# An audio tower on one core: the first normalisation is formed by ACT from PSUM, and DVE applies gamma and beta over pairs of blocks

## The chip, the cores and the metric

The kernel runs on one core of a Trainium2 chip. The metric is the device time of one execution in microseconds (us). TensorE (PE in the profile, PEld for its weight loads) does the matmuls, VectorE (DVE) and ScalarE (ACT) the elementwise work, GpSimd (POOL) a few small operations and the indirect DMAs, SyncE (SP) issues the other DMAs. Each engine works through its own program in order and waits on semaphores.

## What is computed

```python
# tokenizer: patches of 16 time steps, projected, then normalised with gamma and beta
y = einsum('bpi,di->bpd', patches, W) + b
mu, var = mean(y), mean((y - mu)**2)
h = (y - mu) * rsqrt(var + 1e-5) * gamma + beta
# layer 0
h = h + attention(layernorm(h))      # one head, 124 tokens for each batch entry
h = h + ffn(layernorm(h))            # router, top 2 of 6 experts, each of three 256x256 layers
```

There are 128 batch entries of 124 tokens, with 256 features, all in float32. The change concerns the normalisation of the tokenizer only, the line that forms `h`.

## The kernel before

The program has two parts. Part A runs `pipeline(step)`: 36 iterations, `it` = 0 to 35, over 32 groups of four batch entries (a block is one entry: 124 tokens on the partitions, 256 features along them). It is a software pipeline of depth 5. In iteration `it` the stage x0 works on group `it` (tokenizer, its normalisation, the second normalisation), x1 on group `it`-1 (transposed activations, q and v), x2 on `it`-2 (scores, softmax, attention output), x3 on `it`-3 (third normalisation, router), x4 on `it`-4 (top two, places of the tokens in the experts' tables), x5 on `it`-5 (the rest of its scatters). Part B runs `tiles`: 67 tiles of 512 rows through the experts' three layers. It begins when all rows have been scattered, and the change doesn't touch it.

What order the engines follow is written out by hand, in one `step` function per engine; nothing else sets it. The piece around the change, on each engine:

- PE writes the projection of a group into banks 6 and 7, two blocks of 256 columns in each (L550 to L555), and counts `tok_ps`. Later in the same iteration it writes v of the group before into the same banks (L637 to L648), when DVE has read them.
- DVE takes the statistics of the four blocks from PSUM (`statistics(0, ...)`, L889 and L892), which gives mean and variance in `mv`. It goes on with `gates` and `place` (L967) of stage x4. `place` waits for PE's position counts, and PE's transposes of the probabilities (L605) wait for `place`, since both use bank 4.
- POOL forms `rstd1`, the inverse standard deviation, with two small operations (L413, L416), then issues three scatters (L424), and later the same two operations for `rstd2`.
- DVE then forms `y = (x - mean) * gamma` from PSUM (L975, four instructions) and `h = y * rstd + beta` (L981, four), takes the statistics of `h`, and goes on to `nmr` of the second normalisation (L1010) and the attention residual of x2 (L1018).
- ACT copies the transposed probabilities (`pT`, L792), forms `rhT` of the router (L796) and the high half of a weight chunk (L801), and then waits for `nmr` to form the second normalisation `xn1` (L808), which PE transposes (L527) ahead of the scores (L536).

`ln1` counts DVE's steps on a group in stage x0: 25 per group before.

Of the kernel before, what the change touches and what calls it, by code (L numbers as in the profile page):

```python
# [24 lines left out]
ALU = mybir.AluOpType  # L25
# [3 lines left out]
P = 128  # L29
# [29 lines left out]
LN1_N, AV_N, TOPK_N, POS_N = 25, 14, 25, 4  # L59
# [17 lines left out]
def audio_tower(nc, x, tok_w, tok_b, tok_gamma, tok_beta, wq, bq, wk, bk, wv, bv, scale,  # L77
                rw1, rb1, rw2, rb2, eweights, esmall, out):
    with ExitStack() as ctx:
# [39 lines left out]
        nmr = sb("nmr", [P, 2, GB])  # L119
# [37 lines left out]
        with ExitStack() as part_a:  # L157
# [33 lines left out]
            "w_high", "w_low", "dummy_cleared", "xT_high", "xT_low", "xn1T_low", "tok_ps", "ln1", "rstd1", "rstd2", "rstd3", "xn1_ready", "xn1T_ps", "xn1T_sb",  # L191
# [187 lines left out]
        def _(pool):  # L379
# [48 lines left out]
            def step(it, group_of):  # L428
                x0, x2, x4, x5 = (group_of(s) for s in (0, 2, 4, 5))
                if x0:  # L430
                    g, slot, rnd = x0
                    wait_apart(pool, S["ln1"], g * LN1_N + 2 * GB, S["pool_passed"])
                    inverse_std(0, S["rstd1"], g)
                if x5:
                    scatter(x5[0], range(3, 6))
                if x0:
                    g, slot, rnd = x0
                    wait(pool, S["xn1_ready"], g * GB)
                    wait_apart(pool, S["ln1"], g * LN1_N + 6 * GB, S["pool_passed"])
                    inverse_std(1, S["rstd2"], g)  # L440
                if x5:
                    scatter(x5[0], range(6, 8))
                if x2:
                    g, slot, rnd = x2
                    wait(pool, S["xn2_ready"], g * GB)
                    wait_apart(pool, S["av"], g * AV_N + 1 + 3 * GB, S["pool_passed"])
                    inverse_std(2, S["rstd3"], g)
                if x4:
                    g, slot, rnd = x4
                    pool.wait_ge(S["pos"], (g + 1) * POS_N)  # L450
                    pool.wait_ge(S["topk"], (g + 1) * TOPK_N)
                    wait_apart(pool, S["xn2_ready"], (g + 1) * GB, S["pool_passed"])
                    scatter(g, range(3 if g < G - 1 else GB * TOPK))
# [27 lines left out]
        def _(pe):  # L481
# [37 lines left out]
            def step(it, group_of):  # L519
# [19 lines left out]
                if x0:  # L539
# [5 lines left out]
                    for pair in range(2):  # L545
                        bank_read(pe, (S["v_ready"], it - 2, (it - 2) * 2 + pair + 1),
                                  (S["ln1"], it - 1, (it - 1) * LN1_N + 2 * GB + 2 + 2 * pair))
# [89 lines left out]
                if x1:  # L637
                    g, slot, rnd = x1
                    for pair in range(2):
                        bank_read(pe, (S["ln1"], it, it * LN1_N + 2 * GB + 2 + 2 * pair),  # L640
# [61 lines left out]
        def _(act):  # L702
# [26 lines left out]
            def step(it, group_of):  # L729
# [59 lines left out]
                if x2:  # L789
                    g, slot, rnd = x2  # L790
                    act.wait_ge(S["pT_ps"], g + 1)
                    act.activation(pT[0:TOK + 1, :], banks[4][0:TOK + 1, 0:GT], ACT.Identity).then_inc(S["pT_sb"], 1)  # L792
                if x3:
# [66 lines left out]
        def _(v):  # L860
# [21 lines left out]
            def statistics(which, src, s, at, g):  # L882

                for j in range(GB):
                    if which == 0:
                        v.wait_ge(S["tok_ps"], g * 2 + j // 2 + 1)
                    else:
# [35 lines left out]
            def step(it, group_of):  # L923
# [35 lines left out]
                if x4:  # L959
                    gates(*x4)  # L960
                if x4:
# [8 lines left out]
                if x0:  # L970
                    g, slot, rnd = x0
                    at = g * LN1_N
                    v.wait_ge(S["rstd1"], g * 2 + 2)
                    for j in range(GB):
                        v.scalar_tensor_tensor(out=y[R, j, :], in0=embedded(j), scalar=mv[R, 0, j, 0:1],  # L975
                                               in1=gamma_bc[R, :], op0=ALU.subtract, op1=ALU.mult).then_inc(S["ln1"], 1)
                    wait(v, h2_stored[slot], rnd * 16)
                    wait(v, S["xn2_ready"], (g - RING + 1) * GB)
                    for j in range(GB):
                        v.wait_ge(S["ln1"], at + 2 * GB + 1 + j)  # L980
                        v.scalar_tensor_tensor(out=h[R, slot, j, :], in0=y[R, j, :], scalar=rstd[R, 0, j:j + 1],  # L981
                                               in1=beta_bc[R, :], op0=ALU.mult, op1=ALU.add).then_inc(S["ln1"], 1)
                if x0:
                    g, slot, rnd = x0
                    statistics(1, lambda j: h[R, slot, j, :], S["ln1"], g * LN1_N + 4 * GB, g)
# [238 lines left out]
```

## Time and profile before

| | us |
|---|---|
| median of 3 runs | 1405.89 (1405.25 to 1407.78) |
| the profiled execution | 1404.13 |
| its span, first to last instruction | 1402.3 |
| outside the span | 1.8 |

| engine | busy us | share of the span |
|---|---|---|
| PE | 1250.8 | 89% |
| PEld | 1088.5 | 78% |
| DVE | 1057.7 | 75% |
| POOL | 925.9 | 66% |
| ACT | 841.6 | 60% |

Part A fills the span up to about 700 us, part B the rest. A share of busy time is a mean over both, so the rows are best read part by part, and within part A iteration by iteration. Instructions of one engine overlap in the records: the next begins up to 0.1 us before the one ahead ends, so what a series costs is the distance of its starts.

### The profile page before, as it was taken

What the parts mean: (1) busy time and instruction counts of PE and PEld (TensorE: products, weight loads), DVE (VectorE), ACT (ScalarE), POOL (GpSimd) and SP (SyncE); (2) the same over time, 40 slices, a digit from 0 to 9 for tenths busy, and PEclk for the clock granted to TensorE, in tenths of its full rate; (3) what the DMA queues carried; (4) which work ended last, traced back from release to release, by engine and by line L of the source; (5) the groups of instructions that cost most, each with busy time, mean ns of one, the idle gap of its engine ahead of it and who ended that gap; (6) DMA issues with size and microseconds to landing.
All of it is one profiled execution on the core that took longest, in us unless ns stands there. A gap on an engine that the chain in (4) does not pass through costs nothing.

```text
span 1402.3 us, 26155 instructions
## 1 busy us (share of the span) xinstructions
PE 1250.8 (89%) x7888; PEld 1088.5 (78%) x7888; DVE 1057.7 (75%) x3581; ACT 841.6 (60%) x1838; POOL 925.9 (66%) x738
## 2 busy tenths in 40 slices
PE   4898999999999999999609899999999999999993
PEld 3787787888888788877407788888888888888882
DVE  3587888888888888887526577877878777777782
ACT  2376667666666667656305566666666666666661
POOL 1126777777777777777751476766677666766775
PEclk7899999999999999999758999999999999999996
DMA  3023444444444444445566698777967779789764
GB/s 113 27 60 96 105 118 111 116 116 107 111 120 114 107 114 119 115 103 158 165 191 225 178 227 195 123 119 136 290 112 123 119 159 252 127 181 239 120 86 49
DMA packets 141746, 190.95 MB, mean 136 GB/s; under 512 B 37795, under 2 KB 101670, under 8 KB 141606
## 3 DMA queue, kind: packets, MB, share of 16 engines
q0 software_dynamic: 75456, 69.19, 30.9%
q1 hardware_dynamic: 64886, 119.30, 26.9%
q8 instruction: 64, 1.05, 0.3%
q10 hardware_dynamic: 1264, 0.79, 0.2%
q14 instruction: 76, 0.62, 0.1%
HBM read 168.72 MB, written 98.79 MB: 191 GB/s over the span
## 4 chain that ended last, share of the span: by engine, by line
PE 45%; DVE 19%; POOL 15%; issue 7%; DMA 2%; SPq 2%; ACT 1%; POOLq 0%; DVEq 0%; ACTq 0%
PE bank L668 26%; PE bank L690 13%; POOL rstd L416 7%; POOL expert_rows L424 6%; PE bank L658 4%; DVE h L1018 3%; DVE h L981 3%; DVE y L975 3%; DVE xn1T_lo L944 2%; POOL out L474 2%; DVE stats L889 1%; POOL vareps L413 1%; DVE mxi L1056 1%; DVE negmax L938 1%; DMA out<-h 1%
## 5 line engine op out<-in xcount | busy, mean ns | idle before, releaser
L474 POOL DMA_INDIRECT out<-yo,tail x268 | 436.2, 1627 | 236.3 <-issue 148.3
L424 POOL DMA_INDIRECT expert_rows<-rec,row_i x256 | 348.4, 1361 | 77.1 <-issue 63.6
L847 ACT ACTIVATE h2v<-bank,small 128x512 f32<-128x512 f32 x134 | 92.4, 689 | 207.1 <-PE bank L668 207.1
L690 PE MATMUL bank<-w_sb,h_hi 128*128 128x256 f32 x1072 | 210.3, 290 | 2.0 <-DVE h_lo L1140 2.0
L668 PE MATMUL bank<-x_hi,w_sb 128*128 128x512 f32 x536 | 180.3, 398 | 13.8 <-issue 11.3
L668 PE MATMUL bank<-h_hi,w_sb 128*128 128x512 f32 x536 | 177.2, 391 | 0.9 <-DVE h_lo L1140 0.9
L690 PEld LDWEIGHTS bank<-w_sb,h_hi 128*128 128x128 f32 x1072 | 172.6, 193 | 2.8 <-DVE h_lo L1140 2.6
L690 PE MATMUL bank<-w_sb,h_lo 128*128 128x256 f32 x536 | 152.3, 284 | 0.0
L808 ACT ACTIVATE xn<-h,nmr,rstd 124x256 f32<-124x256 f32 x128 | 66.5, 590 | 121.4 <-DVE nmr L1010 121.4
L668 PEld LDWEIGHTS bank<-x_hi,w_sb 128*128 128x128 f32 x536 | 102.6, 191 | 39.1 <-issue 17.9
L853 ACT ACTIVATE yo<-yo,gcol 128x256 f32<-128x256 f32 x268 | 113.9, 498 | 16.9 <-DVE yo L1177 16.9
L413 POOL TENSOR_SCALAR vareps<-mv 124x4 f32<-124x4 f32 x96 | 22.4, 233 | 149.8 <-DVE mv L892 101.5
L416 POOL TENSOR_TENSOR rstd<-vareps,neghalf 124x4 f32<-124x4 f32 x96 | 115.2, 1200 | 8.1 <-POOL vareps L413 0.2
L668 PEld LDWEIGHTS bank<-h_hi,w_sb 128*128 128x128 f32 x536 | 101.0, 188 | 20.8 <-DVE h_lo L1140 1.2
L487 PE MATMUL bank<-tok_proj,xT_hi 128*124 128x256 f32 x512 | 102.9, 294 | 9.2 <-DVE xT_lo L928 9.2
L668 PE MATMUL bank<-x_lo,w_sb 128*128 128x512 f32 x268 | 106.0, 396 | 0.0
L668 PE MATMUL bank<-h_lo,w_sb 128*128 128x512 f32 x268 | 105.2, 393 | 0.0
L690 PEld LDWEIGHTS bank<-w_sb,h_lo 128*128 128x128 f32 x536 | 103.4, 193 | 0.0
L1155 DVE CAST h_hi<-h1v 128x512 fp32r<-128x512 f32 x134 | 61.1, 456 | 54.7 <-ACT h1v L839 54.5
L658 PE MATMUL bank<-ident,xg 128*128 128x128 f32 x536 | 70.5, 275 | 34.0 <-DMA xg<-expert_rows 34.0
L658 PEld LDWEIGHTS bank<-ident,xg 128*128 128x128 f32 x536 | 63.5, 142 | 42.7 <-DMA xg<-expert_rows 34.1
L1140 DVE TENSOR_TENSOR h_lo<-h2v,h_hi 128x512 fp32r<-128x512 f32 x134 | 92.9, 693 | 4.6
(176 smaller groups left out, 3169.7 us busy)
## 6 DMA issues: line engine op xcount, KB each, us to landing
w_sb<-split_weights SPq DMA_DIRECT2D x69, 1536.0 KB, 8.4
xg<-expert_rows SPq DMA_DIRECT2D x67, 530.0 KB, 4.5
out<-h SPq DMA_DIRECT2D x32, 496.0 KB
small<-in_esmall SPq DMA_DIRECT2D x69, 134.0 KB, 10.8
split_weights<-half_w SPq DMA_DIRECT2D x36, 256.0 KB, 3.0
x_in<-in_x SPq DMA_DIRECT2D x32, 250.0 KB, 12.8
raw_w<-in_eweights SPq DMA_DIRECT2D x36, 128.0 KB, 11.5
out<-yo,tail POOLq DMA_INDIRECT x268, 4.1
```

The source lines that it names most:

```text
L416: pool.tensor_tensor(rstd[0:TOK, which, :], vareps[0:TOK, which, :], neghalf[0:TOK, :], ALU.pow).then_inc(ready, 1)
L424: pool.indirect_dma_start(rows_dram, bass.IndirectOffsetOnAxis(ap=row_i[0:TOK, slot, j, k:k + 1], axis=0), rec[0:TOK, slot, j, :], None).t ...
L474: pool.indirect_dma_start(out, bass.IndirectOffsetOnAxis(ap=tail[:, s, j, E8:].bitcast(I32), axis=0), yo[:, ys, j, :], None, compute_op=AL ...
L487: mm = pe.matmul(bank, lhs[a], rhs[b], start=(first and n == 0), stop=(last and n == 2))
L658: mm = pe.transpose(banks[c][:, j * P:(j + 1) * P], xg[:, slot, j, c * P:(c + 1) * P], ident[:])
L668: mm = pe.matmul(banks[bank + m][:], w[:, n, c, wh, m * P:(m + 1) * P], act[:, c, :], start=(c == 0 and p == 0), stop=(c == DC - 1 and p = ...
L690: mm = pe.matmul(banks[6 + b][:, (j % 2) * D:(j % 2 + 1) * D], act[:, c, j * P:(j + 1) * P], w[:, 2, c, wh, :], start=(c == 0 and p == 0), ...
L808: act.activation(xn1[0:TOK, j, :], h[0:TOK, slot, j, :], ACT.Identity, bias=nmr[0:TOK, 0, j:j + 1], scale=rstd[0:TOK, 1, j:j + 1]).then_in ...
L847: act.activation(h2v[:, m, :], banks[4 + m][:], ACT.Relu, bias=small[:, slot, DC + m:DC + m + 1]).then_inc(S["h2_v"], 1)
L853: act.activation(yo[:, ys, j, :], yo[:, ys, j, :], ACT.Identity, scale=gcol[:, ys, j:j + 1]).then_inc(S["y_gated"], 1)
L1140: v.tensor_tensor(lo, val, hi.bitcast(F32), ALU.subtract).then_inc(ready, 1)
L1155: v.tensor_copy(hi[:, m, :], val[:, m, :]).then_inc(s, 1)
```

## The change

ACT now forms `y = x * rstd - mean * rstd` straight from PSUM, one instruction per block with scale and bias per token (L798 of the new kernel, four per group, counted by a new semaphore `xhat`). It stands behind `pT` and ahead of `rhT` in ACT's order. The bias comes from a new small DVE instruction, `nmr[:, 2, :] = -mean * rstd`, which waits for `rstd1` and stands ahead of `place`. DVE's eight instructions over 256 columns become four over 512: `y * gamma` for each pair of blocks (in place), then `+ beta` for each pair into `h`. PE's reuse of banks 6 and 7 waits for `xhat` in place of `ln1`. `ln1` counts 20 steps per group.

```diff
 # ACT, step
+                if x0:
+                    act.wait_ge(S["rstd1"], g * 2 + 2)
+                    act.wait_ge(S["ln1"], g * LN1_N + 2 * GB + 1)
+                    for j in range(GB):
+                        act.activation(y[0:TOK, j, :], banks[6 + j // 2][0:TOK, (j % 2) * D:(j % 2 + 1) * D],
+                                       ACT.Identity, bias=nmr[0:TOK, 2, j:j + 1], scale=rstd[0:TOK, 0, j:j + 1]
+                                       ).then_inc(S["xhat"], 1)
 # DVE, step, behind gates and ahead of place
+                if x0:
+                    g, slot, rnd = x0
+                    v.wait_ge(S["rstd1"], g * 2 + 2)
+                    v.scalar_tensor_tensor(out=nmr[R, 2, :], in0=mv[R, 0, :, 0], scalar=-1.0, in1=rstd[R, 0, :],
+                                           op0=ALU.mult, op1=ALU.mult).then_inc(S["ln1"], 1)
 # DVE, step, behind place
-                    v.wait_ge(S["rstd1"], g * 2 + 2)
-                    for j in range(GB):
-                        v.scalar_tensor_tensor(out=y[R, j, :], in0=embedded(j), scalar=mv[R, 0, j, 0:1],
-                                               in1=gamma_bc[R, :], op0=ALU.subtract, op1=ALU.mult).then_inc(S["ln1"], 1)
                     wait(v, h2_stored[slot], rnd * 16)
                     wait(v, S["xn2_ready"], (g - RING + 1) * GB)
-                    for j in range(GB):
-                        v.wait_ge(S["ln1"], at + 2 * GB + 1 + j)
-                        v.scalar_tensor_tensor(out=h[R, slot, j, :], in0=y[R, j, :], scalar=rstd[R, 0, j:j + 1],
-                                               in1=beta_bc[R, :], op0=ALU.mult, op1=ALU.add).then_inc(S["ln1"], 1)
+                    for i in range(2):
+                        pair = slice(2 * i, 2 * i + 2)
+                        wide = [TOK, 2, D]
+                        v.wait_ge(S["xhat"], g * GB + 2 * i + 2)
+                        v.tensor_tensor(y[R, pair, :], y[R, pair, :], gamma_bc[R, :].unsqueeze(1).to_broadcast(wide),
+                                        ALU.mult).then_inc(S["scaled"], 1)
+                    for i in range(2):
+                        pair = slice(2 * i, 2 * i + 2)
+                        v.wait_ge(S["scaled"], g * 2 + i + 1)
+                        v.tensor_tensor(h[R, slot, pair, :], y[R, pair, :], beta_bc[R, :].unsqueeze(1).to_broadcast(wide),
+                                        ALU.add).then_inc(S["ln1"], 1)
```

How DVE's program reads in a full iteration, from the end of `gates` to the statistics of `h`, before (each row is an instruction or a run of equal ones; in brackets the semaphores it waits for):

```order
L1086 TENSOR_SCALAR tokid<-tokid 124x4
L967 TENSOR_TENSOR place<-bank,place 124x40 [waits pos,pos_ps]
L975 SCALAR_TENSOR_TENSOR y<-bank,mv,gamma_bc 124x256 [waits rstd1]
L975 SCALAR_TENSOR_TENSOR y<-bank,mv,gamma_bc 124x256 x3
L981 SCALAR_TENSOR_TENSOR h<-y,rstd,beta_bc 124x256 [waits ln1,xn2_ready,h2_stored2]
L981 SCALAR_TENSOR_TENSOR h<-y,rstd,beta_bc 124x256 [waits ln1] x3
L889 BN_STATS stats<-h 124x6 [waits ln1] x4
```

and the same place of DVE's program after the change:

```order
L1104 TENSOR_SCALAR tokid<-tokid 124x4
L974 SCALAR_TENSOR_TENSOR nmr<-mv,rstd 124x4 [waits rstd1]
L982 TENSOR_TENSOR place<-bank,place 124x40 [waits pos,pos_ps]
L994 TENSOR_TENSOR y<-y,gamma_bc 124x512 [waits xhat,xn2_ready,h2_stored2]
L994 TENSOR_TENSOR y<-y,gamma_bc 124x512 [waits xhat]
L999 TENSOR_TENSOR h<-y,beta_bc 124x512 [waits scaled] x2
L899 BN_STATS stats<-h 124x6 [waits ln1] x4
```

The wait for `rstd1` has moved ahead of `place`, eight instructions have become four, and the first two of them wait for ACT.

ACT's program in a full iteration, from the q projection's copies to the second normalisation, before:

```order
L792 ACTIVATE pT<-bank 125x496 [waits pT_ps]
L796 ACTIVATE rhT<-bank,rb_col 128x496 [waits rh_ps]
L801 ACTIVATE half_w<-raw_w 128x256 [waits w_stored2,raw_loaded2]
L808 ACTIVATE xn<-h,nmr,rstd 124x256 [waits xn1T_ps,rstd2,ln1]
L808 ACTIVATE xn<-h,nmr,rstd 124x256 x3
```

and after:

```order
L787 ACTIVATE qT<-bank,score_col 128x496 [waits q_ps] x2
L792 ACTIVATE pT<-bank 125x496 [waits pT_ps]
L798 ACTIVATE y<-bank,nmr,rstd 124x256 [waits ln1,rstd1]
L798 ACTIVATE y<-bank,nmr,rstd 124x256 x3
L804 ACTIVATE rhT<-bank,rb_col 128x496 [waits rh_ps]
L809 ACTIVATE half_w<-raw_w 128x256 [waits w_stored2,raw_loaded2]
```

The four new instructions stand behind `pT` (a copy that waits for PE's transposes, `pT_ps`), and `rhT` and `half_w` come behind them.

## Rows read from the trace of the kernel before

**Rows 1.** The page: busy time of the engines, and the chain that ended last.

```profile
PE 1250.8 (89%) x7888; PEld 1088.5 (78%) x7888; DVE 1057.7 (75%) x3581; ACT 841.6 (60%) x1838; POOL 925.9 (66%) x738
...
PE 45%; DVE 19%; POOL 15%; issue 7%; DMA 2%; SPq 2%; ACT 1%; POOLq 0%; DVEq 0%; ACTq 0%
```

**Rows 2.** Busy by stretch: PE, PEld, DVE, ACT, POOL, PE's clock, DMA share, GB/s.

```profile
300.00:400.00 100.00, 93.51 (x643) 80.46 (x642) 86.85 (x386) 66.11 (x161) 76.33 (x71) 1.00 0.44 113
...
50.00:54.00 4.00, 3.22 (x12) 2.43 (x13) 0.43 (x1) 4.00 (x9) 0.00 (x0) 0.50 0.40 109
68.00:72.00 4.00, 2.22 (x15) 1.46 (x14) 2.76 (x10) 2.55 (x6) 1.13 (x2) 1.00 0.19 69
132.00:135.00 3.00, 2.81 (x14) 2.46 (x13) 1.67 (x10) 2.80 (x7) 2.35 (x4) 0.50 0.62 125
```

**Rows 3.** Timeline of DVE, one iteration: start, duration, instruction, [idle before, releaser].

```profile
341.04 0.20 DVE L967 TENSOR_TENSOR place<-bank,place 124x40 f32<-124x40 f32 x1 [0.25 <-PE bank L596]
341.36 1.66 DVE L975 SCALAR_TENSOR_TENSOR y<-bank,mv,gamma_bc 124x256 f32<-124x256 f32 x4
...
344.51 1.41 DVE L889 BATCH_NORM_STATS2 stats<-h 124x6 f32<-124x256 f32 x4
345.83 0.41 DVE L892 BATCH_NORM_AGGREGATE mv<-stats 124x2 f32<-124x6 f32 x4
...
353.25 0.16 DVE L933 SCALAR_TENSOR_TENSOR nmr<-mv,rstd 124x4 f32<-124x4 f32 x1 [0.94 <-POOL rstd L416]
353.43 0.68 DVE L938 TENSOR_REDUCE negmax<-bank 124x4 f32<-124x496 f32 x1
354.02 1.25 DVE L944 TENSOR_TENSOR xn1T_lo<-xn1T,xn1T_hi 128x496 fp32r<-128x496 f32 x2
```

**Rows 4.** Timeline of ACT, the same iteration.

```profile
342.04 0.58 ACT L792 ACTIVATE pT<-bank 125x496 f32<-125x496 f32 x1 [0.72 <-PE bank L605]
...
348.02 2.08 ACT L808 ACTIVATE xn<-h,nmr,rstd 124x256 f32<-124x256 f32 x4 [3.34 <-DVE nmr L1010]
```

**Rows 5.** Timeline of PE around transposes and scores: the same iteration, then three others.

```profile
348.82 0.28 PE L487 MATMUL bank<-v_proj,xn1T_lo 128*124 128x256 f32 x1
...
350.16 0.75 PE L527 MATMUL bank<-ident,xn 124*128 124x124 f32 x5 [0.17 <-ACT xn L808]
351.42 1.97 PE L536 MATMUL bank<-xn1T,qT 128*124 128x124 f32 x16 [0.52 <-DVE logits L1034]
...
50.73 2.68 PE L527 MATMUL bank<-ident,xn 124*128 124x124 f32 x8 [3.37 <-ACT xn L808]
...
130.10 0.65 PE L527 MATMUL bank<-ident,xn 124*128 124x124 f32 x2 [2.70 <-DVE h L1018]
...
608.96 3.12 PE L536 MATMUL bank<-xn1T,qT 128*124 128x124 f32 x16 [0.84 <-DVE logits L1034]
```

**Rows 6.** Timeline of DVE, one instruction in successive iterations.

```profile
585.34 0.16 DVE L1010 SCALAR_TENSOR_TENSOR nmr<-mv,rstd 124x4 f32<-124x4 f32 x1 [0.60 <-POOL rstd L416]
...
605.04 0.16 DVE L1010 SCALAR_TENSOR_TENSOR nmr<-mv,rstd 124x4 f32<-124x4 f32 x1 [0.61 <-POOL rstd L416]
...
626.44 0.16 DVE L1010 SCALAR_TENSOR_TENSOR nmr<-mv,rstd 124x4 f32<-124x4 f32 x1 [0.61 <-POOL rstd L416]
```

**Rows 7.** Timeline of POOL, the iteration of rows 3.

```profile
340.21 1.11 POOL L416 TENSOR_TENSOR rstd<-vareps,neghalf 124x4 f32<-124x4 f32 x1
...
346.44 0.23 POOL L413 TENSOR_SCALAR vareps<-mv 124x4 f32<-124x4 f32 x1 [0.19 <-issue]
```

**Rows 8.** Durations by form, DVE: count, busy us, mean ns, idle before.

```profile
L1177 DVE TENSOR_TENSOR yo<-bank,small 128x512 f32<-128x512 f32 x134 | 85.7, 681 | 0.0
```

**Rows 9.** Timelines of DVE and ACT in iteration 2, which has no stage x4.

```profile
62.75 1.66 DVE L975 SCALAR_TENSOR_TENSOR y<-bank,mv,gamma_bc 124x256 f32<-124x256 f32 x4 [1.58 <-POOL rstd L416]
...
63.38 0.57 ACT L792 ACTIVATE pT<-bank 125x496 f32<-125x496 f32 x1
63.84 0.42 ACT L801 ACTIVATE half_w<-raw_w 128x256 fp32r<-128x256 f32 x1
```

More of the change, by code:

```diff
@@ L56 @@
 SMALL = 2 * DC + D + E8
-LN1_N, AV_N, TOPK_N, POS_N = 25, 14, 25, 4
+LN1_N, AV_N, TOPK_N, POS_N = 20, 14, 25, 4
 ADDED = 16 * TB
@@ L118, in audio_tower @@
         rstd = sb("rstd", [P, 3, GB])
-        nmr = sb("nmr", [P, 2, GB])
+        nmr = sb("nmr", [P, 3, GB])
         negmax, rinv = sb("negmax", [P, GB]), sb("rinv", [P, GB])
@@ L190, in audio_tower @@
             "tok_loaded", "const_loaded", "pool_const", "dve_const", "invs", "proj_high", "proj_low", "bias_zero",
-            "w_high", "w_low", "dummy_cleared", "xT_high", "xT_low", "xn1T_low", "tok_ps", "ln1", "rstd1", "rstd2", "rstd3", "xn1_ready", "xn1T_ps", "xn1T_sb",
+            "w_high", "w_low", "dummy_cleared", "xT_high", "xT_low", "xn1T_low", "tok_ps", "ln1", "rstd1", "rstd2", "rstd3", "xhat", "scaled", "xn1_ready", "xn1T_ps", "xn1T_sb",
             "fold_ps", "fold_sb", "folded", "bv_ready", "bv_placed", "q_ps", "q_sb", "v_ps", "v_ready", "scores_ps", "score_max", "probs_ready", "pT_ps", "pT_sb",
@@ L438, in step @@
                     wait(pool, S["xn1_ready"], g * GB)
-                    wait_apart(pool, S["ln1"], g * LN1_N + 6 * GB, S["pool_passed"])
+                    wait_apart(pool, S["ln1"], g * LN1_N + 4 * GB + 3, S["pool_passed"])
                     inverse_std(1, S["rstd2"], g)
@@ L546, in step @@
                         bank_read(pe, (S["v_ready"], it - 2, (it - 2) * 2 + pair + 1),
-                                  (S["ln1"], it - 1, (it - 1) * LN1_N + 2 * GB + 2 + 2 * pair))
+                                  (S["xhat"], it - 1, (it - 1) * GB + 2 + 2 * pair))
                         for j in (0, 1):
@@ L639, in step @@
                     for pair in range(2):
-                        bank_read(pe, (S["ln1"], it, it * LN1_N + 2 * GB + 2 + 2 * pair),
+                        bank_read(pe, (S["xhat"], it, it * GB + 2 + 2 * pair),
                                   (S["v_ready"], it - 2, (it - 2) * 2 + pair + 1))
@@ L886, in statistics @@
                         v.wait_ge(S["tok_ps"], g * 2 + j // 2 + 1)
+                    elif which == 1:
+                        v.wait_ge(s, at - 1 + j // 2)
                     else:
@@ L972, in step @@
                     at = g * LN1_N
-                    v.wait_ge(S["rstd1"], g * 2 + 2)
-                    for j in range(GB):
-                        v.scalar_tensor_tensor(out=y[R, j, :], in0=embedded(j), scalar=mv[R, 0, j, 0:1],
-                                               in1=gamma_bc[R, :], op0=ALU.subtract, op1=ALU.mult).then_inc(S["ln1"], 1)
                     wait(v, h2_stored[slot], rnd * 16)
                     wait(v, S["xn2_ready"], (g - RING + 1) * GB)
-                    for j in range(GB):
-                        v.wait_ge(S["ln1"], at + 2 * GB + 1 + j)
-                        v.scalar_tensor_tensor(out=h[R, slot, j, :], in0=y[R, j, :], scalar=rstd[R, 0, j:j + 1],
-                                               in1=beta_bc[R, :], op0=ALU.mult, op1=ALU.add).then_inc(S["ln1"], 1)
+                    for i in range(2):
[9 more added lines that the diff above has]
+                                        ALU.add).then_inc(S["ln1"], 1)
                 if x0:
                     g, slot, rnd = x0
-                    statistics(1, lambda j: h[R, slot, j, :], S["ln1"], g * LN1_N + 4 * GB, g)
+                    statistics(1, lambda j: h[R, slot, j, :], S["ln1"], g * LN1_N + 2 * GB + 3, g)
                 if x4:
```

1 line of the change is left out of this document (added).

## Prediction

> **What bounds the kernel now.** I began with the page's busy shares and its chain [rows 1]. PE is busy 89%, yet the chain gives PE only 45%, and DVE and POOL together 34%. Those shares mix the two parts, so busy time by stretch comes next. In part A PE is busy 93.5% and DVE 86.9% of 100 us, ACT 66%, at a granted clock of 1.00, which is 2.4 GHz [rows 2]. Two engines so full leave open which of them sets the pace. The timelines of one iteration answer it. DVE's idle times there are short and each is ended by POOL or PE: 0.25 us before `place`, 0.94 before the third normalisation's `nmr` [rows 3], 0.61 before the second's [rows 6]. So the loop runs from DVE to POOL (rstd) and back, with DVE busy in between. ACT waits 3.34 us for DVE ahead of `xn1` [rows 4], and PE in turn waits for ACT in the transposes and for DVE ahead of the scores [rows 5]. The pace is 19.70 us per iteration, the distance of one DVE instruction from 585.34 to 605.04 [rows 6]. Around the change, what ends last is DVE's own series, released by `rstd1`: that one ends at 341.32 [rows 7], `y` begins at 341.36, and the statistics of `h` begin at 344.51 [rows 3]. These 3.19 us lie on the path in each of 32 groups. Nothing behind them can run ahead: the statistics feed POOL, which feeds `nmr`, then `xn1`, then PE's transposes.
>
> **The change, part by part.** The question is when the statistics of `h` begin if `rstd1` ends at 341.32.
>
> *DVE's work.* Eight instructions cost 344.51 - 341.36 = 3.15 us [rows 3]. Four of 124x512 replace them. The nearest row takes 681 ns, with 512 columns and a broadcast operand, though from PSUM [rows 8]. Two of 496 columns take 1.25 us where the first begins the second after 0.58 [rows 3], so with 512 columns I count 0.60 from start to start. Four cost 2.40. `nmr` takes 0.16, of which about 0.09 is its share in a row of others. The work shrinks by 3.15 - 2.40 - 0.09 = 0.66 us per group.
>
> *The wait for `rstd1` moves ahead of `place`.* `place` started at 341.04. Now it comes behind `nmr`, which can't start before 341.36: `place` starts at 341.45, 0.41 later. PE's probability transposes and ACT's `pT` wait for it, so `pT` starts at 342.04 + 0.41 = 342.45 [rows 3, 4]. On PE the router product, the attention output and v, queued behind those transposes, move by the same 0.41, to an end of v at 349.10 + 0.41 = 349.51 [rows 5]. That is covered, since `xn1` will be later still.
>
> *ACT's four instructions* stand behind `pT`. From `pT` to the next ACT instruction it is 63.84 - 63.38 = 0.46 us [rows 9], so the first starts at 342.91. The nearest row for their price is `xn1`, with the same shape, scale and bias per token: four take 2.08 us, 0.50 from start to start and 0.58 for the last [rows 4]. Its source is SBUF, here it is PSUM; I take the same. Two are ready at 343.99, four at 344.99. `rhT` is queued behind them and starts near 344.9; what waits for it is PE's logits product, which stands behind the attention output and hardly notices.
>
> *Where the sum lands.* DVE has finished `place` at 341.65 and may do nothing until 344.06: **some 2.4 us idle**, a wait that wasn't there. The first gamma instruction starts at 344.06, the second, held by the fourth of ACT, at 345.05, the betas at 345.65 and 346.25, and the statistics at 346.85. Before it was 344.51, so they come 2.34 us later.
>
> *Is any of it given back?* POOL's next step started at 346.44, 0.2 behind the end of DVE's `mv` at 346.24 [rows 3, 7], so it moves by the full 2.34. `nmr`, `xn1`, the transposes, the scores and the third statistics hang on it one behind the other. The 28 full iterations (`it` 4 to 31) cost 28 x 2.34 = 65.5 us.
>
> *The first four iterations* have no `place` to wait for. In `it` = 2 `y` began at 62.75, so the statistics began 3.15 later, at 65.90. ACT would begin its four at 63.84 [rows 9] and end 2.08 later at 65.92; the second gamma then starts at 65.98 and the statistics 1.80 later at 67.78: 1.9 us more. I take this for all four: 7.5.
>
> Together 73 us. Part B starts that much later and is otherwise the same.
>
> *PE's clock.* In a steady iteration PE idles between v and the scores 0.17 us twice (one of the two rows is shown) and 0.52 once, 0.86 in all [rows 5], at full clock [rows 2]. Afterwards v ends at 349.51 and the first transpose waits until about 351.1, which is 1.6 more, some 2.5 us. The trace has this place at other sizes. With 3.37 us idle ahead of the transposes eight of them took 2.68 us at a clock of 0.50, which is 1.2 GHz [rows 2, 5]. With 2.70 (at 130.10) the clock fell too; with 1.78 idle of the 4 us from 68 on it stayed at 1.00 [rows 2, 5]. At 609 it fell after an iteration hardly quieter than its neighbours (0.84 in place of 0.52), and the scores took 3.12 us where 1.97 is usual [rows 5]. So 2.5 us lie near the value at which it fell, and beyond those at which it mostly held. A fall costs the loop, because `negmax` on DVE starts right at the end of the scores (353.39 and 353.43) [rows 3, 5]: that iteration took 626.44 - 605.04 = 21.40 in place of 19.70, 1.7 more [rows 6]. I take 1.3, since part of it came through `place`, where PE now has 0.4 us in hand. I count a fall in three of four full iterations: 21 x 1.3 = 27 us. The bounds are 0 (no fall) and 28 x 1.7 = 48.
>
> The Trainium skill, "TensorE: Matmul & The Clock Gate", section "HAM oscillation — how this bites in real kernels", describes a kernel in which a wait of PE in every round let the clock fall anew each time. [...]
>
> **The sum.** 1404.1 of the profiled execution + 73 + 27 = 1504.1. The median lay 1.8 above the profiled execution, so **1506 us**.
>
> **The rivals.**
>
> *The clock holds.* Only the wait for ACT is paid: 1405.9 + 73 = 1479. For it speaks that 1.78 us idle did no harm; against it the fall at 609. If ACT's reads of PSUM were as cheap as its 256 columns without scale and bias per token, 0.42 us [rows 9], the four would end about 0.3 earlier, and the time would be 1470.
>
> *The clock falls in each iteration at full price.* 1405.9 + 73 + 48 = 1527. For it speaks that the quiet stretch recurs at the same place; against it PE's slack at `place`.
>
> *The shorter DVE work is the gain.* If DVE's work sets the pace of part A, 0.66 us less in each of 32 groups gives 21: 1385. It decides at DVE's idle time ahead of the gamma instructions: below 0.66 us per group the change gains, above it loses. For it speaks DVE's 86.9% [rows 2]. Against it: ACT would have to be through with two blocks by 342.3, 1.0 us after `rstd1`, with 1.1 us of its own work to do and `pT` ahead of it. The Trainium skill, "VectorE: DVE Perf Modes", section "The TRN2 errata — SBUF-src ops pay a fixed extra latency per instruction", advises tiles of 512 elements and more, so that a fixed part is paid less often. By that page alone this rival would win; the trace shows the saving in work too, but the place has no use for it.
>
> *The loop gives the delay back.* DVE's three idle times, 0.25 + 0.61 + 0.94 = 1.8 us, would vanish if POOL and PE ran ahead during the new wait: 28 x 1.8 = 50 of the 73, so 1429. Against it: both waits for POOL follow DVE's own statistics, and can't end earlier than these allow.
>
> *How the numbers follow.* Forecast 1506 (its own range 1489 to 1517): 0.55. Clock holds, 1479: 0.22. Falls at full price, 1527: 0.15. Gain, 1385: 0.04. Given back, 1429: 0.04. The range takes in the clock that holds with the cheaper ACT instruction, and ends at the full price: 1470 to 1527. It leaves out the last two cases and about half of the dearest. A measurement of this kernel can tell about 0.2%, 2.8 us, from no change. Faster 0.04, within it 0.01, slower 0.95.
>
> **What would show it.** In the profile after: DVE idle some 2.4 us before the first gamma instruction (L994), ended by ACT's `y`, and 0.3 to 0.4 before the second; ACT's four about 0.5 apart, the first 0.46 behind `pT`; from `nmr` to the next iteration's `nmr` 22.0 us where the clock holds and 23.3 where it falls; a granted clock between 200 and 600 us near 0.9; part B as long as before. The forecast would be wrong if DVE hardly waited for ACT, if iterations took 22.0 us throughout (then the clock term goes), if ACT's instructions from PSUM were much dearer or cheaper than 0.5 us from start to start, or if POOL no longer ended DVE's later waits, so that the delay was given back.

## The result and the profile after

The changed kernel takes 1496.2 us (median of 4 runs, 1491.5 to 1498.7), against 1405.6 us for the kernel before in the same comparison: a ratio of 1.064, with a 95% interval of 1.061 to 1.067. The profiled execution took 1491.5 us with a span of 1489.5, 87.2 us more than the span before. That is slower, as forecast, and 10 us less than the 1506 predicted. The kernel before, timed again for the experiments, had medians of 1401.8, 1404.0 and 1403.3 us, so times of different comparisons are best set side by side by their ratios.

The page shows who fills less of the span now. Beside [rows 1], PE, DVE and POOL have a smaller share of it, and the chain hardly names DVE any more:

```profile
PE 1284.2 (86%) x7888; PEld 1116.0 (75%) x7888; DVE 1039.9 (70%) x3485; ACT 899.2 (60%) x1966; POOL 936.7 (63%) x738
...
PE 41%; POOL 4%; issue 3%; DMA 2%; ACT 1%; DVE 1%; POOLq 0%; SPq 0%; ACTq 0%
```

DVE's work did shrink, from 1057.7 to 1039.9 us, in a kernel that takes 90 us longer. The chain adds up to only about half of the span here, so it does not answer what bounds part A. Busy time by stretch does (columns as in [rows 2]: us, PE, PEld, DVE, ACT, POOL, clock, DMA share, GB/s):

```profile
300.00:400.00 100.00, 85.74 (x558) 73.16 (x557) 73.86 (x321) 66.45 (x158) 69.46 (x63) 0.95 0.38 99
```

DVE went from 86.9% to 73.9%, and the clock from 1.00 to 0.95. No engine is full. DVE's timeline in one iteration (start, duration, instruction, idle before and its releaser), answering [rows 3]; the clock held up to the last row shown:

```profile
451.32 0.16 DVE L974 SCALAR_TENSOR_TENSOR nmr<-mv,rstd 124x4 f32<-124x4 f32 x1 [0.56 <-POOL rstd L416]
451.41 0.20 DVE L982 TENSOR_TENSOR place<-bank,place 124x40 f32<-124x40 f32 x1
454.03 1.50 DVE L994 TENSOR_TENSOR y<-y,gamma_bc 124x512 f32<-124x512 f32 x2 [2.42 <-ACT y L798]
455.45 1.29 DVE L999 TENSOR_TENSOR h<-y,beta_bc 124x512 f32<-124x512 f32 x2
456.65 1.40 DVE L899 BATCH_NORM_STATS2 stats<-h 124x6 f32<-124x256 f32 x4
...
459.96 0.16 DVE L1028 SCALAR_TENSOR_TENSOR nmr<-mv,rstd 124x4 f32<-124x4 f32 x1 [0.61 <-POOL rstd L416]
```

There is the wait that wasn't there before: 2.42 us, ended by ACT's `y`. From the end of `rstd1` (450.18 + 1.11 = 451.29) to the statistics of `h` it is now 5.36 us, where it was 3.19. ACT and POOL in the same iteration, answering [rows 4, 7]:

```profile
452.40 0.58 ACT L792 ACTIVATE pT<-bank 125x496 f32<-125x496 f32 x1 [1.15 <-PE bank L605]
452.88 1.93 ACT L798 ACTIVATE y<-bank,nmr,rstd 124x256 f32<-124x256 f32 x4
454.68 0.69 ACT L804 ACTIVATE rhT<-bank,rb_col 128x496 f32<-128x496 f32 x1
```

```profile
450.18 1.11 POOL L416 TENSOR_TENSOR rstd<-vareps,neghalf 124x4 f32<-124x4 f32 x1
451.53 1.43 POOL L424 DMA_INDIRECT expert_rows<-rec,row_i  x1 [0.24 <-issue]
453.27 1.32 POOL L424 DMA_INDIRECT expert_rows<-rec,row_i  x1 [0.30 <-issue]
454.89 1.84 POOL L424 DMA_INDIRECT expert_rows<-rec,row_i  x1 [0.30 <-issue]
458.57 0.23 POOL L413 TENSOR_SCALAR vareps<-mv 124x4 f32<-124x4 f32 x1 [1.84 <-issue]
```

ACT starts its four 0.48 us behind `pT` and needs 1.93 us for them. Before, POOL began the next `vareps` 0.19 us behind its third scatter; now it idles 1.84 us there. The third scatter takes 1.84 instead of 1.32, which matters further down.

PE around the transposes and the scores, answering [rows 5], in two successive iterations, the first with the clock held and the second with a fall:

```profile
439.13 0.64 PE L527 MATMUL bank<-ident,xn 124*128 124x124 f32 x2 [1.53 <-DVE h L1036]
...
441.71 1.97 PE L536 MATMUL bank<-xn1T,qT 128*124 128x124 f32 x16 [0.53 <-DVE logits L1052]
...
460.99 0.64 PE L527 MATMUL bank<-ident,xn 124*128 124x124 f32 x2 [1.54 <-DVE h L1036]
461.80 0.33 PE L527 MATMUL bank<-ident,xn 124*128 124x124 f32 x1 [0.17 <-ACT xn L816]
462.29 0.75 PE L527 MATMUL bank<-ident,xn 124*128 124x124 f32 x5 [0.17 <-ACT xn L816]
463.57 3.50 PE L536 MATMUL bank<-xn1T,qT 128*124 128x124 f32 x16 [0.54 <-DVE logits L1052]
```

and the busy time by stretch beside those scores, with the granted clock in the third column from the end:

```profile
442.00:444.00 2.00, 2.00 (x21) 2.00 (x20) 1.05 (x4) 1.96 (x5) 1.76 (x2) 1.00 0.71 147
464.00:466.00 2.00, 2.00 (x12) 2.00 (x12) 0.63 (x2) 2.00 (x5) 1.76 (x2) 0.50 0.71 129
```

PE waits 1.54 us ahead of the transposes, and 0.17, 0.17 and 0.54 behind, 2.4 us in all. In the second of the two iterations the scores run at 0.50, which is 1.2 GHz, and take 3.50 us where 1.97 is usual. The quiet is the same 2.4 us in the first, so its size alone doesn't decide on a fall.

One DVE instruction (L1028, the `nmr` of the second normalisation) in successive iterations, answering [rows 6]:

```profile
438.11 0.16 DVE L1028 SCALAR_TENSOR_TENSOR nmr<-mv,rstd 124x4 f32<-124x4 f32 x1 [0.61 <-POOL rstd L416]
459.96 0.16 DVE L1028 SCALAR_TENSOR_TENSOR nmr<-mv,rstd 124x4 f32<-124x4 f32 x1 [0.61 <-POOL rstd L416]
...
483.64 0.16 DVE L1028 SCALAR_TENSOR_TENSOR nmr<-mv,rstd 124x4 f32<-124x4 f32 x1 [0.61 <-POOL rstd L416]
```

That is 21.85 us without a fall and 23.68 with one. Over the 27 distances from iteration 4 to iteration 31, this instruction's starts (115.45 to 736.15) show 8 near 21.9, one of 25.2 and 18 between 22.8 and 23.8, mean 23.4. The clock falls 20 times in this stretch. The one of 25.2 stands where the kernel before has one of 22.8.

### The profile page after: what moved, and what is told of

Its sections match the earlier page's. It is cut to its first block, busy times and chain, and to the rows that moved or that the text cites. A ratio compares the mean times of both kernels' runs of the same rounds, so it can differ in the third digit from the quotient of the medians.

```text
span 1489.5 us, 26219 instructions
## 1 busy us (share of the span) xinstructions
PE 1284.2 (86%) x7888; PEld 1116.0 (75%) x7888; DVE 1039.9 (70%) x3485; ACT 899.2 (60%) x1966; POOL 936.7 (63%) x738
## 4 chain that ended last, share of the span: by engine, by line
PE 41%; POOL 4%; issue 3%; DMA 2%; ACT 1%; DVE 1%; POOLq 0%; SPq 0%; ACTq 0%
PE bank L668 24%; PE bank L690 12%; PE bank L658 4%; POOL expert_rows L424 3%; POOL out L474 1%; DMA out<-yo,tail 1%; DMA expert_rows<-rec,row_i 1%; ACT rec L762 0%; PE bank L568 0%; DMA xg<-expert_rows 0%; POOL rstd L416 0%; PE bank L487 0%; POOLq L79 0%; DVE h L1036 0%; ACT xn2T L776 0%
## 5 line engine op out<-in xcount | busy, mean ns | idle before, releaser
L424 POOL DMA_INDIRECT expert_rows<-rec,row_i x256 | 359.7, 1405 | 76.9 <-issue 72.0
L527 PE MATMUL bank<-ident,xn 124*128 124x124 f32 x256 | 57.1, 308 | 67.6 <-DVE h L1036 43.9
L536 PE MATMUL bank<-xn1T,qT 128*124 128x124 f32 x512 | 90.6, 353 | 15.5 <-DVE logits L1052 15.5
L536 PEld LDWEIGHTS bank<-xn1T,qT 128*124 128x124 f32 x512 | 84.9, 261 | 21.3 <-issue 21.3
L527 PEld LDWEIGHTS bank<-ident,xn 124*128 124x128 f32 x256 | 31.2, 144 | 92.1 <-DVE h L1036 50.1
```

The lines of the kernel that those rows point to most:

```text
L424: pool.indirect_dma_start(rows_dram, bass.IndirectOffsetOnAxis(ap=row_i[0:TOK, slot, j, k:k + 1], axis=0), rec[0:TOK, slot, j, :], None).t ...
L527: mm = pe.transpose(banks[1 + c][:, j * TOK:(j + 1) * TOK], xn1[0:TOK, j, c * P:(c + 1) * P], ident[0:TOK, 0:TOK])
L536: mm = pe.matmul(banks[5][0:TOK, j * TOK:(j + 1) * TOK], qT[:, c, j * TOK:(j + 1) * TOK], xn1T[:, g % 2, c, j * TOK:(j + 1) * TOK], start= ...
```

## The experiments

The theory: DVE waits for ACT in every group; ACT is late because it stands behind `pT`, which stands behind PE's transposes and `place`; and the wait opens a quiet stretch on PE in which the clock falls. The rivals: something else makes the long iterations, PE or POOL is the real bound, or DVE's shorter work is a gain that only the wait hides. In each experiment the kernel before was timed on the same chip.

**Filling PE's quiet stretch.** Seven matmuls without a purpose behind v:

```diff
                         mm.then_inc(S["v_ps"], 1)
+                    pe.wait_ge(S["q_sb"], g * 2 + 1)
+                    for n in range(7):
+                        pe.matmul(banks[0][:, 0:GT], ones_r[:], xn1T_hi[:, 0, :], start=True, stop=True)
```

> The changed kernel, with seven matmuls of 496 columns added on PE behind v, into bank 0, whose result nobody reads. They fill most of the 1.9 us in which PE idles ahead of the transposes. Theory (the new wait of DVE costs 2.2 us per iteration, and PE's clock falls in 21 of 28 full iterations cost some 1.3 each on top): no falls are left in part A's full iterations, all of them take 21.9 us, and the time is 1496 - 25 = 1471. Rival 1 (the longer iterations have another cause, DMA or POOL, and the low clock only goes with it): iterations of 23.2 to 23.8 us remain and the time stays at 1496. Rival 2 (the filling itself delays the transposes): all iterations become longer than 21.9.

Measured: 1474.0 us, a ratio of 1.051 (1.047 to 1.055). Busy time by stretch, with the clock at 1.00 where the changed kernel has 0.95, and PE's timeline in one iteration:

```profile
400.00:500.00 100.00, 92.58 (x618) 78.61 (x617) 76.79 (x332) 67.28 (x161) 71.92 (x65) 1.00 0.39 101
```

```profile
449.31 1.73 PE L651 MATMUL bank<-xn1T_hi,ones_r 128*128 128x496 f32 x7
...
453.59 1.97 PE L536 MATMUL bank<-xn1T,qT 128*124 128x124 f32 x16 [0.53 <-DVE logits L1055]
```

PE does more and the kernel is faster, by 22 us from median to median and by 18 when each is taken against the kernel before timed beside it (90.6 and 72.3 us above it). The usual iteration is 21.87 us, with the wait for ACT as it was, and the clock falls at two places of the full iterations (134 and 554 us) in place of 20. So the falls were a cost of their own. Over the 27 distances the time beyond 27 x 21.87 went from 30.2 to 7.4 us; with 18 falls fewer that is 1.3 us for each, and by the medians it is 1.0 to 1.2. A few distances of 22.2 and 22.75 us are left in which the clock held, so the long iterations of the changed kernel aren't wholly the clock's.

**ACT's four instructions ahead of `pT`.** The block `if x0:` with `act.activation(y[...])` moves ahead of the block with `pT`, nothing else:

```diff
+                if x0:
+                    act.wait_ge(S["rstd1"], g * 2 + 2)
+                    act.wait_ge(S["ln1"], g * LN1_N + 2 * GB + 1)
...
                 if x2:
                     g, slot, rnd = x2
                     act.wait_ge(S["pT_ps"], g + 1)
...
-                if x0:
-                    act.wait_ge(S["rstd1"], g * 2 + 2)
-                    act.wait_ge(S["ln1"], g * LN1_N + 2 * GB + 1)
```

> The changed kernel, with ACT's four new instructions ahead of pT instead of behind it. Theory: they start about 0.1 us behind nmr instead of behind place, PE's transposes and pT, 1.35 us earlier. DVE's idle time ahead of the first gamma instruction falls from 2.1-2.7 to about 0.9 us, the full iteration from 21.86 to 20.5; pT moves 0.4 us later, which the router product and the attention output cover. PE's quiet stretch shrinks as much, so the clock falls seldom (0 to 8 times). 28 x 1.35 = 38, plus 15 to 27 of the clock: 1496 - 60 = 1436 (1430 to 1450). Rival (the attention output now waits for pT and takes the place of the wait removed): iteration above 21.2 us, time above 1460.

Measured: 1434.6 us, a ratio of 1.022 (1.018 to 1.026). The usual iteration takes 20.57 us. DVE's timeline, then ACT's:

```profile
397.33 0.16 DVE L974 SCALAR_TENSOR_TENSOR nmr<-mv,rstd 124x4 f32<-124x4 f32 x1 [0.56 <-POOL rstd L416]
397.42 0.20 DVE L982 TENSOR_TENSOR place<-bank,place 124x40 f32<-124x40 f32 x1
398.75 1.50 DVE L994 TENSOR_TENSOR y<-y,gamma_bc 124x512 f32<-124x512 f32 x2 [1.13 <-ACT y L794]
```

```profile
397.59 1.93 ACT L794 ACTIVATE y<-bank,nmr,rstd 124x256 f32<-124x256 f32 x4 [0.32 <-DVE nmr L974]
399.40 0.59 ACT L800 ACTIVATE pT<-bank 125x496 f32<-125x496 f32 x1
```

The wait shrinks from 2.42 to 1.13 us, the iteration by 1.3, and the clock falls three times in the full iterations, at 129, 357 and 607. Two thirds of the loss (6.4% before the move, 2.2% after it) came from the place of four instructions in ACT's order. The last third can't go that way: even first in line, ACT needs 1.0 us for two blocks while DVE has nothing to do.

**`nmr` behind `place`,** where `y` waited for `rstd1` before the change:

```diff
-                    v.scalar_tensor_tensor(out=nmr[R, 2, :], in0=mv[R, 0, :, 0], scalar=-1.0, in1=rstd[R, 0, :],
-                                           op0=ALU.mult, op1=ALU.mult).then_inc(S["ln1"], 1)
...
                                     carry.unsqueeze(1).to_broadcast([TOK, GB + 1, E8]), ALU.add).then_inc(S["pos"], 1)
...
+                    v.scalar_tensor_tensor(out=nmr[R, 2, :], in0=mv[R, 0, :, 0], scalar=-1.0, in1=rstd[R, 0, :],
+                                           op0=ALU.mult, op1=ALU.mult).then_inc(S["ln1"], 1)
```

> The changed kernel, with nmr and its wait for rstd1 behind place instead of ahead of it on DVE. Theory: place, PE's transposes and pT start 0.4 us earlier, and with them ACT's four instructions: iteration 21.45 us where the clock holds, 28 x 0.4 = 11 us less, 1485. The clock goes on falling in most iterations. Rival (nmr, not pT, holds ACT's first instruction): no change, 1496.

Measured: 1479.3 us, a ratio of 1.056 (1.050 to 1.061). DVE's timeline:

```profile
446.43 0.20 DVE L977 TENSOR_TENSOR place<-bank,place 124x40 f32<-124x40 f32 x1 [0.23 <-PE bank L596]
446.77 0.16 DVE L983 SCALAR_TENSOR_TENSOR nmr<-mv,rstd 124x4 f32<-124x4 f32 x1
```

Iterations of 21.44 and of 23.05 us alternate, the clock falling in every second one. The shorter iteration is 0.42 us less than 21.86, as the theory has it (0.4). The total, 11 us forecast and 17 measured (13 by the ratios), has a second part: the clock falls 15 times in place of 20. The iterations with and without a fall have the same quiet on PE, 2.4 us, so here too something besides its size decides.

**DVE's shorter work alone.** Without ACT's four instructions: DVE multiplies the raw projection by gamma straight from PSUM.

```diff
-                        v.wait_ge(S["xhat"], g * GB + 2 * i + 2)
-                        v.tensor_tensor(y[R, pair, :], y[R, pair, :], gamma_bc[R, :].unsqueeze(1).to_broadcast(wide),
+                        v.tensor_tensor(y[R, pair, :], banks[6 + i][R, :].rearrange("p (b n) -> p b n", b=2), gamma_bc[R, :].unsqueeze(1).to_broadcast(wide),
```

> The changed kernel without ACT's four instructions: DVE multiplies the raw projection in PSUM by gamma and adds beta, both over pairs, after the same wait for rstd1 ahead of place. Mean and standard deviation are left out of the first normalisation. This times DVE's shorter work without the wait for ACT. Theory: 0.6 us less per full iteration than before the change (four instructions at 0.6 start to start against 3.15 us for eight, and nmr 0.1): iteration 19.1 us, 1405.6 - 32 x 0.6 = 1386 (1383 to 1392). Rival (place 0.4 us later delays PE, which then takes over): iteration 19.7 or more, 1405 or more.

Measured: 1415.7 us, a ratio of 1.009 (1.006 to 1.013). The theory missed: with less work for DVE and no wait for ACT the kernel is no faster than before. Most iterations take 19.7 to 20.2 us, and some 20.6 to 21.3. The numbers are those of the rival, a `place` that comes 0.4 us later; whether its cause is right too, the run after next shows. POOL's timeline and DVE's next `nmr` show another cause:

```profile
399.90 1.43 POOL L424 DMA_INDIRECT expert_rows<-rec,row_i  x1 [0.24 <-issue]
401.64 1.38 POOL L424 DMA_INDIRECT expert_rows<-rec,row_i  x1 [0.30 <-issue]
403.32 1.32 POOL L424 DMA_INDIRECT expert_rows<-rec,row_i  x1 [0.30 <-issue]
404.67 0.44 POOL L413 TENSOR_SCALAR vareps<-mv 124x4 f32<-124x4 f32 x1
```

```profile
406.27 0.17 DVE L1019 SCALAR_TENSOR_TENSOR nmr<-mv,rstd 124x4 f32<-124x4 f32 x1 [1.25 <-POOL rstd L416]
```

DVE's `mv` ends at 404.06, but POOL comes from its scatters only at 404.64, and DVE idles 1.25 us instead of 0.61. Before the change both ended at the same moment, DVE's `mv` at 346.24 [rows 3] and POOL's third scatter at 346.25:

```profile
344.93 1.32 POOL L424 DMA_INDIRECT expert_rows<-rec,row_i  x1 [0.30 <-issue]
```

In the median iteration `mv` ends 4.37 us behind `rstd1`, 0.55 earlier than before (4.92); the scatters end 4.94 us behind it (4.92 before). So nothing that only shortens DVE's series there could have gained anything. One more wait is new here. DVE's wait for the store of an older `h` now stands ahead of the first of the four instructions, not between the two halves. The list of waits (us in total, times, longest us) has it:

```profile
DVE y L985 <- DMA out<-h: 4.7, 5, 1.3
```

That the whole kernel is slower isn't POOL's doing, though. In the two profiled executions part A is level: the last scatter starts at 723.8 us, and at 724.2 before. The 10.5 us more of span lie behind it, in part B, whose program is the same (689.0 against 678.1 us). This kernel forms other values, which may give the tokens other places; whether that lengthens part B wasn't followed. The same stretch takes 676 to 684 us in all other kernels here.

**One scatter moved, in the kernel before.** To test POOL as the second bound:

```diff
-                    scatter(x5[0], range(3, 6))
+                    scatter(x5[0], range(4, 6))
...
-                    scatter(g, range(3 if g < G - 1 else GB * TOPK))
+                    scatter(g, range(4 if g < G - 1 else GB * TOPK))
```

> The kernel before, with one of POOL's eight scatters per iteration moved: two instead of three stand between rstd1 and rstd2, four instead of three behind rstd3. Control for the next run. If POOL's three scatters and DVE's own series end together between rstd1 and rstd2 (346.25 and 346.24 in the trace of before), freeing POOL there brings nothing by itself, and the fourth scatter makes POOL 0.2 to 0.4 us late for rstd1: iteration 19.9 to 20.1, time 1402 + 28 x 0.3 = 1410 (1405 to 1415). If POOL alone was the bound there, the iteration becomes shorter than 19.6 and the time falls below 1400.

Measured: 1407.5 us, a ratio of 1.003 (1.001 to 1.005). The usual iteration is 19.84 us, 0.15 more than before. POOL's timeline:

```profile
386.21 1.31 POOL L424 DMA_INDIRECT expert_rows<-rec,row_i  x1 [0.30 <-issue]
389.34 0.23 POOL L413 TENSOR_SCALAR vareps<-mv 124x4 f32<-124x4 f32 x1 [1.82 <-issue]
```

POOL is free 1.82 us early, and the stretch from the end of `rstd1` to DVE's second `nmr` is still 6.50 us, as before. So POOL alone was not the bound. The 0.15 us come from the other side, where the fourth scatter stands: from DVE's second `nmr` to the end of the next `rstd1` it is 13.35 us, where it was 13.19.

**The same scatter moved, with DVE's shorter work.**

> The kernel of e4_dve_only (mean and standard deviation left out of the first normalisation) with the same scatter moved. Theory: in e4 DVE's shorter series gained nothing since POOL's three scatters hold the second inverse standard deviation; with one of them moved the 0.6 us come out, less 0.3 for POOL's later rstd1: iteration 19.3 to 19.5 against 19.77 in e4, time 1395 to 1402 against 1415.7. Rival (PE, or place coming 0.4 us later, is what held e4): iteration 19.8 or more, 1415 or more.

Measured: 1404.7 us, a ratio of 1.002 (1.000 to 1.004), against 1.009 without the move. The commonest iteration is 19.32 us. Each edit alone brings nothing, both together take some 0.5 us off the iterations of either. So two series end together ahead of the second inverse standard deviation, DVE's and POOL's. The rival of the last run but one is out, since `place` is as late as there. The time came out a little above the 1395 to 1402 expected. In the profiled execution (1399.1 us) part A is 11.4 us shorter than before, with the last scatter at 712.8 us, and part B 6.3 us longer; besides, two iterations in five take 19.6 to 20.6 us. What lengthens these was not followed.

**Half of the change.** ACT forms blocks 2 and 3 only, ahead of `pT`; DVE meanwhile forms blocks 0 and 1 in the old way and then does the second pair over 512 columns:

```diff
-                    for j in range(GB):
+                    for j in (2, 3):
...
+                    for j in (0, 1):
+                        v.scalar_tensor_tensor(out=y[R, j, :], in0=embedded(j), scalar=mv[R, 0, j, 0:1],
+                                               in1=gamma_bc[R, :], op0=ALU.subtract, op1=ALU.mult).then_inc(S["scaled"], 1)
...
+                        v.scalar_tensor_tensor(out=h[R, slot, j, :], in0=y[R, j, :], scalar=rstd[R, 0, j:j + 1],
+                                               in1=beta_bc[R, :], op0=ALU.mult, op1=ALU.add).then_inc(S["ln1"], 1)
...
+                    v.wait_ge(S["xhat"], g * 2 + 2)
+                    v.tensor_tensor(y[R, 2:4, :], y[R, 2:4, :], gamma_bc[R, :].unsqueeze(1).to_broadcast(wide),
+                                    ALU.mult).then_inc(S["scaled"], 1)
...
+                    v.tensor_tensor(h[R, slot, 2:4, :], y[R, 2:4, :], beta_bc[R, :].unsqueeze(1).to_broadcast(wide),
+                                    ALU.add).then_inc(S["ln1"], 1)
```

The statistics of `h` for blocks 0 and 1 stand around that last instruction.

> Half of the change: ACT forms only blocks 2 and 3, ahead of pT, while DVE forms blocks 0 and 1 from PSUM in the old way; DVE then does the second pair over 512 columns. DVE needs no wait for ACT (two instructions end 1.0 us behind nmr, DVE is busy with its own four for 1.6), and its series is some 0.2 us shorter than before. Theory A (POOL's scatters hold the second inverse standard deviation): the iteration stays at 19.7 to 19.8 us and the time within 0.4% of the kernel before, 1402 to 1407. Theory B (DVE's series alone is the bound): 19.5 us, 1397. Either way the 60 to 90 us of the full change are gone, since only the wait cost them.

Measured: 1417.7 us, a ratio of 1.009 (1.007 to 1.011). The wait for ACT is gone and with it most of the loss, but neither theory has this number: more than half of the iterations take 20.0 to 20.5 us. DVE's timeline and POOL's:

```profile
390.56 0.88 DVE L991 SCALAR_TENSOR_TENSOR y<-bank,mv,gamma_bc 124x256 f32<-124x256 f32 x2 [0.72 <-DMA out<-h]
```

```profile
391.49 1.53 POOL L424 DMA_INDIRECT expert_rows<-rec,row_i  x1 [0.30 <-issue]
393.32 1.62 POOL L424 DMA_INDIRECT expert_rows<-rec,row_i  x1 [0.30 <-issue]
```

Two more causes are possible, then: DVE's wait for the stored `h`, and scatters of 1.5 and 1.6 us where 1.32 is usual. The long ones lie beside DVE's 512-column instructions, which read two operands from SBUF. The next two runs take one cause each.

**The waits for `h` behind the first two instructions** (the diff is against the run before):

```diff
-                    wait(v, h2_stored[slot], rnd * 16)
-                    wait(v, S["xn2_ready"], (g - RING + 1) * GB)
                     for j in (0, 1):
                         v.scalar_tensor_tensor(out=y[R, j, :], in0=embedded(j), scalar=mv[R, 0, j, 0:1],
                                                in1=gamma_bc[R, :], op0=ALU.subtract, op1=ALU.mult).then_inc(S["scaled"], 1)
+                    wait(v, h2_stored[slot], rnd * 16)
+                    wait(v, S["xn2_ready"], (g - RING + 1) * GB)
```

> The kernel of e7_split_blocks with one thing moved: DVE's waits for the stored h and for the third normalisation (which guard the buffer h) stand behind its first two instructions instead of ahead of them, as they did before the change. In e7 DVE waited there for the store of h in 8 iterations, 6.0 us in all. Theory: these waits go to near 0, the time falls by 5 to 6 us to 1412; the iteration stays at 20.1, since POOL's second scatter (1.47 us on average where 1.32 is usual) is not touched. Rival (the split order itself is the cost): no change, 1417.

Measured: 1414.0 us, a ratio of 1.007 (1.005 to 1.009). The wait fell from 6.0 to 2.6 us, and the commonest iteration is 20.14 us. So the order of the waits is worth some 3 us, less than the 5 to 6 expected; the ratio fell by 0.2%, and the intervals of the two runs overlap. The waits in that run:

```profile
DVE h L995 <- DMA out<-h: 2.6, 4, 0.9
```

**And the pair left in PSUM** (the diff is against the run before; PE's waits, changed to match, are left out):

```diff
-                        act.activation(y[0:TOK, j, :], banks[6 + j // 2][0:TOK, (j % 2) * D:(j % 2 + 1) * D],
+                        act.activation(banks[6 + j // 2][0:TOK, (j % 2) * D:(j % 2 + 1) * D], banks[6 + j // 2][0:TOK, (j % 2) * D:(j % 2 + 1) * D],
...
-                    v.tensor_tensor(y[R, 2:4, :], y[R, 2:4, :], gamma_bc[R, :].unsqueeze(1).to_broadcast(wide),
+                    own = banks[7][R, :].rearrange("p (b n) -> p b n", b=2)
+                    v.tensor_tensor(own, own, gamma_bc[R, :].unsqueeze(1).to_broadcast(wide),
...
-                    v.tensor_tensor(h[R, slot, 2:4, :], y[R, 2:4, :], beta_bc[R, :].unsqueeze(1).to_broadcast(wide),
+                    v.tensor_tensor(h[R, slot, 2:4, :], own, beta_bc[R, :].unsqueeze(1).to_broadcast(wide),
```

> The kernel of e8 with one more thing changed: ACT leaves the second pair's normalised values in PSUM (bank 7, in place) and DVE's two instructions over 512 columns read them there, so each has one operand from SBUF instead of two. Theory (a DVE instruction with two SBUF operands holds up POOL's scatter beside it, and the scatters end last ahead of the second inverse standard deviation): all scatters take 1.32 us but the first, the iteration goes from about 20.1 to 19.7 us, the time to 1404 (1400 to 1407), level with the kernel before. Rival (the longer scatters have another cause): iteration 20.1, time as e8. PE's v into bank 7 now waits for DVE's last read, which ends about 2.9 us behind nmr, ahead of its turn.

Measured: 1405.3 us, a ratio of 1.0005 (0.999 to 1.002), as the theory had it. The commonest iteration is 19.82 us and the scatters are back to their length. The second one behind `rstd1`, beside DVE's wide instructions, took 1.64 us on average in the run before and takes 1.33 now, which is the 0.3 us of the iteration. DVE's two instructions cost the same in both (686 and 674 ns on average, then 693 and 674), so it isn't they that became faster. POOL by groups, between 150 and 600 us, with two SBUF operands and with one (count, busy us, mean ns, idle and what ended it):

```profile
L424 POOL DMA_INDIRECT expert_rows<-rec,row_i x178 | 249.9, 1404 | 50.0 <-issue 44.2 <-DVE h L995 5.8
```

```profile
L424 POOL DMA_INDIRECT expert_rows<-rec,row_i x180 | 245.2, 1362 | 50.6 <-issue 44.6 <-DVE h L995 6.1
```

The kernel before has 1361 ns in the same stretch and the changed one 1420. The Trainium skill, "SBUF — State Buffer", section "🔬 SBUF: two separate sides", says that a DVE instruction with two SBUF inputs holds the port pair that it shares with GpSimd, against a GpSimd operation that reads SBUF. These runs agree in part, with 1.64 us against 1.33 for the second scatter. But other DVE instructions with two SBUF operands, `h` over 256 columns in the kernel before and `xn1T_lo` over 496 columns in all the kernels, have scatters of the usual length beside them, but for one of 1.73 us. What else it takes stays open.

The best version of the half change is level with the kernel before, and none tried beats it.

## Why the prediction was right

**The bound.** That DVE's series around `rstd1` lies on the path held: the distance from `rstd1` to the statistics grew by 2.17 us and the iteration by 2.16 (21.86 against 19.70). The reading was incomplete in one point. It takes DVE's series as the only one that ends last ahead of the second `rstd`, and doesn't look at POOL's third scatter, which ends 0.01 us behind it. For a longer DVE series that made no difference; for a shorter one it does: less DVE work alone left the usual iteration at 19.8 us, and with a scatter moved it came to 19.32.

**The terms.** `place` 0.4 us later: the run with `nmr` behind it gave 0.42 back. ACT 0.46 behind `pT`: 0.48. DVE's idle time of 2.4 us: 2.42. The work of DVE shrank by 0.55 us behind `rstd1`, not 0.66, since `place` now lies there too. The mis-sized term is ACT's price from PSUM: 0.45 us from start to start (1.93 for four) where I took 0.50 from the row with an SBUF source. So the full iteration cost 2.16, not 2.34, and 28 of them 60.5 in place of 65.5 us. The first four iterations came to 7.0 us (86.61 before, 93.62 now, for the same instruction in iteration 3), against 7.5, but that was luck: 1.1, 1.0, 1.0 and 3.9 instead of 1.9 each. Of the 3.9 us, 1.4 lie ahead of `rstd1`, in an iteration in which the clock had fallen (at 74.0 us), which the term didn't hold.

**The clock.** 21 falls at 1.3 us were forecast, 27 us. The profile has 20 between iterations 4 and 31, in 19 of the 27 distances, where the iterations beyond 21.86 us add 30.5, less the 8.2 that the kernel before had beyond 19.69: 22.3. The filled kernel puts the price at 1.0 to 1.3 each. The mechanism held; that the count came so close is partly luck, since the prediction had only bounds (0 and 28) and a guess between them, and since falls came and stayed away with the same quiet of 2.4 us. The clock of the stretch was 0.95, where 0.9 was expected. The rival in which the clock holds (1479) was that kernel, in effect, at 1474. The rival of a fall in every iteration (1527) is out: eight of 27 distances had none.

**The sum, against the span.** 9.2 us up to `nmr` of iteration 4 (7.0 and the first full distance), 58.6 in 27 distances at 2.17, 22.3 in longer iterations, and -2.8 from there to the end: 87.2 in all, but for rounding. The end varied by several us between kernels whose part B is the same, so the last term is not explained further.

**The other rivals.** The gain from shorter work was given 1385 and a point from which it decides, 0.66 us of idle time. That point was wrong. In the run without ACT's part DVE didn't idle ahead of them and the kernel still gained nothing: POOL took over. The delay was not given back by the later waits either: 0.61 ahead of `nmr` before and after [rows 6], and 0.94 ahead of the third normalisation's.

## What to carry to other kernels

When work moves from a busy engine to an idle one, ask where in the other engine's order it will stand and what that order is waiting for just then; the idle share says nothing of this, and moving the four instructions ahead of one copy was worth two thirds of the loss here. Where two engines' series end within 0.01 us of each other, as here, look for the second one: shortening the first gains nothing until the other is shortened too. And compare part by part, not only the totals: one run here was 10 us slower with the changed part level. A new wait can cost twice, once for itself and once for the clock of the TensorE that it leaves quiet.

## What the runs showed of the hardware

PE with seven useless matmuls per iteration made the kernel 18 to 22 us faster, since the clock stayed at 2.4 GHz; without them a quiet of 2.4 us per iteration, broken by short transposes, let it fall to 1.2 in 19 of 27 iterations. In others it held with the same quiet, and with `nmr` behind `place` it fell in every second one. In the kernel before, with 0.86 us there, it fell in two of the full ones.

ACT's instruction over 124x256 with scale and bias per token takes 571 ns from PSUM and 587 ns from SBUF (medians), and from start to start 0.45 against 0.50 us.

POOL's indirect DMA issue, 1.32 us as a rule (1.43 for the first behind `rstd`), took 1.83 us as a median beside the changed kernel's DVE instructions over 512 columns with two SBUF operands, and 1.71 in the split kernel; with one of the operands in PSUM it took 1.32.
